# Loading in order of need, preparing weights late, and reordering the opening steps of two expert stages

## What is computed

```
x += tanh(gx[0]) * attention0(c, norm(x))     # 8 heads, rotary keys
x += tanh(gf[0]) * experts0(norm(x))          # top 2 of 8 linear experts
x += tanh(gx[1]) * attention1(c, norm(x))     # 16 heads
x += tanh(gf[1]) * spiking1(norm(x))          # relu^2, then spike counts
x += tanh(gx[2]) * attention2(c, c, norm(x))  # one head, with biases
x += tanh(gf[2]) * experts2(norm(x))          # softmax router, top 2 of 8, gelu, hidden 192
x += tanh(gx[3]) * attention3(norm(x), c, c)  # one head, causal
x += tanh(gf[3]) * quantised3(norm(x))        # 4-bit weights in blocks of 32, 16-bit activations
```

## Time and profile before

| | us |
|---|---|
| three runs: median (lowest to highest) | 2214.97 (2210.58 to 2215.29) |
| the profiled execution | 2211.95 |
| its span | 2210.1 |
| PE busy | 1922.3 (87%) |
| DVE busy | 1670.8 (76%) |
| ACT busy | 1296.7 (59%) |
| POOL busy | 262.2 (12%) |

### The profile page before, as it was taken

How to read it: one execution, slowest core, us unless ns; L and a number is a source line. 1 busy time by engine, 2 the same in 40 slices (tenths; PEclk the granted TensorE clock), 3 DMA queues, 4 the chain that set the end, 5 groups by cost and what they waited for, 6 DMA issues and landing times. The chain is left out here.

```text
span 2210.1 us, 48541 instructions
## 1 busy us (share of the span) xinstructions
PE 1922.3 (87%) x17853; PEld 1474.7 (67%) x17853; DVE 1670.8 (76%) x4753; ACT 1296.7 (59%) x3156; POOL 262.2 (12%) x551
## 2 busy tenths in 40 slices
PE   2999999999978989999989896999999986499708
PEld 2778777777757987877757674677777765244308
DVE  2778777778748968999968695766666578787894
ACT  1777777777752218888856463544544345317844
POOL 0111111111101101111111142000000022200000
PEclk8999999999988998999989897999999998699959
DMA  6111111111105541111100011222122111002452
GB/s 183 45 45 45 45 45 45 45 45 45 45 18 225 221 174 31 31 32 32 31 3 1 10 58 49 84 109 78 77 78 92 63 49 30 1 0 86 171 199 77
DMA packets 114381, 151.53 MB, mean 69 GB/s; under 512 B 46538, under 2 KB 95075, under 8 KB 110051
## 3 DMA queue, kind: packets, MB, share of 16 engines
q1 hardware_dynamic: 108152, 145.72, 20.3%
q10 hardware_dynamic: 5994, 2.70, 0.5%
HBM read 110.11 MB, written 21.50 MB: 60 GB/s over the span
## 5 line engine op out<-in xcount | busy, mean ns | idle before, releaser
L1728 ACT ACTIVATE arena<-banks,b1c 128x512 f32<-128x512 f32 x192 | 131.7, 687 | 168.0 <-PE banks L1603 167.9
L1690 DVE TENSOR_TENSOR arena<-arena 128x512 f32<-128x512 f32 (+1 forms) x256 | 170.6, 685 | 66.1 <-ACT arena L1728 63.0
L606 ACT ACTIVATE arena<-banks,arena 128x128 f32<-128x128 f32 x512 | 180.1, 371 | 1.3 <-DVE arena L556 1.3
L1613 PEld LDWEIGHTS banks<-w2a,arena 128*128 128x128 f32 x1024 | 124.1, 192 | 28.6 <-issue 28.6
L858 PE MATMUL banks<-we,arena 128*128 128x128 f32 x1024 | 131.7, 282 | 4.4 <-DVE arena L922 0.5
L481 PE MATMUL banks<-arena,wk 128*128 128x128 f32 x1024 | 134.6, 286 | 1.1 <-DVE arena L578 1.1
L520 PE MATMUL banks<-wv,arena 128*128 128x512 f32 x256 | 132.0, 598 | 0.0
L481 PEld LDWEIGHTS banks<-arena,wk 128*128 128x128 f32 x1024 | 122.3, 196 | 12.5 <-issue 11.0
L858 PEld LDWEIGHTS banks<-we,arena 128*128 128x128 f32 x1024 | 121.1, 193 | 13.0 <-DVE arena L922 12.8
L1613 PE MATMUL banks<-w2a,arena 128*128 128x128 f32 x1024 | 124.7, 275 | 0.0
L1603 PE MATMUL banks<-arena,w1s 128*128 128x512 f32 x256 | 121.7, 610 | 0.0
(11 more groups left out here) (264 smaller groups left out, 5034.6 us busy)
## 6 DMA issues: line engine op xcount, KB each, us to landing
arena<-coef_scratch SPq DMA_DIRECT2D x32, 2048.0 KB, 7.1
arena<-arena SPq DMA_DIRECT2D x256, 64.0 KB, 2.0
gated_scratch<-arena SPq DMA_DIRECT2D x16, 768.0 KB, 3.2
arena<-gated_scratch SPq DMA_DIRECT2D x16, 768.0 KB, 4.2
arena<-z1T_scratch SPq DMA_DIRECT2D x128, 64.0 KB, 2.3
arena<-in_ctx_turned SPq DMA_DIRECT2D x32, 256.0 KB, 2.9
arena<-in_ctx SPq DMA_DIRECT2D x64, 64.0 KB, 2.1
z1T_scratch<-arena SPq DMA_DIRECT2D x64, 64.0 KB, 1.5
```

Source lines behind the costliest of these rows:

```text
L606: act.activation(prob[:, o, c * P:(c + 1) * P], ps[:, SCORES + o, c * P:(c + 1) * P], ACT.Exp, bias=low[:, o, c:c + 1], accum_out=total[:, ...
L1613: mm = pe.matmul(ps[:, OUT + g.par, j * D:(j + 1) * D], hT[g.par][:, c, j * P:(j + 1) * P], w, start=c == 0, stop=c == CHUNKS2 - 1)
L1690: dve.tensor_tensor(hT[g.par][rows, c, :], hT[g.par][rows, c, :], wide_coef[g.par][rows, e, :], ALU.mult).then_inc(s["scaled"].sem, 1)
L1728: act.activation(hT[g.par][:, c, :], ps[:, HID + c % NHID, :], ACT.Gelu, bias=k.b1c[:, c:c + 1])\
```

## The change

Six things are changed; tile sizes, loops in the steady state and arithmetic stay.

1. **Loads.** SP loads the constants, context tile 0, then wk and wq. ACT loads x tiles 0 to 3, the affine columns (now one transfer), wv, wo, the gates, then x tiles 4 to 15. x tiles 16 to 39, x tiles 40 to 63 and the other 31 weight transfers are issued by SP in attention0, one after each tile's swap. PE and DVE wait for the seven first weight transfers only before their first use; DVE waits for each part of `x` at its first tile; every engine waits for the 31 others at the start of experts0.
2. **Host layout.** Five weights come already transposed, bv already widened, the eight affine vectors and b1 in one array each. Their PE transposes and ACT copies go.
3. **Folded weights** (six matrix products, six copies) are computed on PE and ACT at the start of spiking1.
4. **Dequantising** runs on DVE in experts2, at the end of the step in which group 8 is routed; PE and ACT turn and copy the result at the start of attention3, one matrix after another through one PSUM bank.
5. **experts0, first four steps.** DVE computes the new group's shift before `top_two` instead of after it; ACT copies coefT first, then norms, and only then computes the sigmoids. PE transposes the coefficients before the logits, in all steps.
6. **experts2, first three steps.** DVE runs statistics one step ahead and norms first; the weighing of chunks 0 to 8 comes before the bias sum; PE transposes group 1 early and computes the first three hidden chunks of group 0 one step earlier.

```diff
+        load_x(act, 0)
+        for dst, src in first_act:
+            act.dma_start(dst, src).then_inc(k.first_loaded, 16)
+        load_x(act, 1)
+        ready(act)
...
+    def load_rest(sp, n):
+        if n < 2:
+            load_x(sp, 2 + n)
+        elif n - 2 < len(rest):
+            sp.dma_start(*rest[n - 2]).then_inc(k.rest_loaded, 16)
...
 # attention0, sync
                 for r in range(0, P, 32):
                     sp.dma_start(kr[r:r + 32, :], kc[r ^ 32:(r ^ 32) + 32, :]).then_inc(swapped.at(t), 16)
+                k.load_rest(sp, t.idx)
 # attention0, vector
+                if t.idx == 0:
+                    k.ready(dve)
                 dve.wait_ge(*f["xT_psum"](t))
...
 # Folds.tensor; spiking1 calls it before its steps, Folds.scalar likewise
+        pe.matmul(ps[:, 7, 0:D], w2[:, 2 * D:3 * D], w2[:, 0:D], start=True, stop=True)
...
+        pe.wait_ge(k.folded_sb, 6)
...
+def dequantised_turned(k, pe):
+    pe.wait_ge(k.dequant, 10)
+    for w in range(3):
+        if w:
+            pe.wait_ge(k.turned_sb, w)
+        flat = k.q_deq[:, w].rearrange("p b i -> p (b i)")
+        for c in range(CHUNKS3):
+            mm = pe.transpose(k.psum[:, 7, c * P:(c + 1) * P], flat[:, c * P:(c + 1) * P], k.ident)
+        mm.then_inc(k.turned, 1)
+    pe.wait_ge(k.turned_sb, 3)
...
 # experts0, vector
+            if new and not at(0):
+                shifts(new)
             if far:
                 top_two(far)
+            if new and at(0):
+                shifts(new)
...
 # experts2, tensor
+            if at(3) and not nxt:
+                t_front(pe, at(3))
+            if far and far.idx == 0:
+                hidden(far, 0)
             for q in range(GROUP):
-                if nxt:
+                if nxt and (q or nxt.idx):
                     hidden(nxt, 3 * q)
...
 # experts2, vector
+        def opening(at):
+            nxt, far, new = at(1), at(2), at(3)
+            if new.idx == 0:
+                statistics(new)
+            normalised(new)
+            if far:
+                scores(far)
+                routing(far)
+            if not nxt:
+                statistics(at(4))
+            if nxt:
+                dve.wait_ge(*coef_spread(nxt))
+                for c in (0, 3, 6):
+                    weigh(nxt, c)
+            if far:
+                biased(far)
+            if nxt:
+                weigh(nxt, 9)
...
+            if far and far.idx == G // 2:
+                weights3.vector(dve)
```

More of the change, by code:

```diff
@@ L865, in body @@
                 outputs(g, 0)
+            if g := at(2):
+                pe.wait_ge(*s["coef"](g))
+                if g.has(1):
+                    pe.wait_ge(*s["ct_sb"](g.back(1)))
+                pe.transpose(ps[0:COLS, COEFT, 0:P], coef[g.par], k.ident).then_inc(s["ct_psum"].sem, 1)
             if g := at(3):
@@ L952, in scalar, with shares @@
     def scalar(act):
-        def body(at):
-            if g := at(3):
-                act.wait_ge(*s["gap"](g))
-                if g.has(1):
-                    act.wait_ge(*s["part"](g.back(1)))
-                for n in range(2):
-                    act.activation(share[:, n], gap, ACT.Sigmoid, scale=2.0 * n - 1.0).then_inc(s["share"].sem, 1)
+        def shares(g):
+            act.wait_ge(*s["gap"](g))
+            if g.has(1):
+                act.wait_ge(*s["part"](g.back(1)))
+            for n in range(2):
+                act.activation(share[:, n], gap, ACT.Sigmoid, scale=2.0 * n - 1.0).then_inc(s["share"].sem, 1)
+        def body(at):
             if g := at(2):
@@ L971, in body @@
                                    bias=shift[:, j:j + 1]).then_inc(f["xhat_ready"].sem, 1)
+            if at(3) and not at(0):
+                shares(at(3))
+            if g := at(4):
                 act.wait_ge(*f["xT_psum"](g))
@@ L1691, in weigh, with statistics, normalised, biased @@
                                       ALU.mult).then_inc(s["scaled"].sem, 1)
+        def statistics(g):
+            for j in range(GROUP):
+                d_front.stats(dve, g, j)
+            d_front.aggr(dve, g)
+        def normalised(g):
+            for j in range(GROUP):
+                d_front.xhat(dve, g, j)
+        def biased(g):
+            dve.wait_ge(*s["b2_psum"](g))
+            dve.tensor_tensor(rows_of(g), ps[:, LOGITS, :], rows_of(g), ALU.add).then_inc(s["b2_added"].sem, 1)
+        def opening(at):
[16 more added lines that the diff above has]
+                weigh(nxt, 9)
         def body(at):
             old, nxt, far, new = at(-1), at(1), at(2), at(3)
+            if not at(0) and not old:
+                opening(at)
+                return
             if far:
@@ L1702, in body @@
             if new:
-                for j in range(GROUP):
-                    d_front.stats(dve, new, j)
-                d_front.aggr(dve, new)
+                statistics(new)
             if nxt:
@@ L1709, in body @@
             if new:
-                for j in range(GROUP):
-                    d_front.xhat(dve, new, j)
+                normalised(new)
             if far:
@@ L1744, in body @@
                     act.activation(coefT[0:EXPERTS, :], ps[0:EXPERTS, COEFT, :], ACT.Copy).then_inc(s["ct_sb"].sem, 1)
-            if at(3):
+            if at(3) and (nxt or not far):
                 a_front(act, at(3))
@@ L2140 @@
     arrays, args = {}, {}
[L2141 to L2142 removed]
+    for name, a in laid_out(inputs).items():
         a = np.ascontiguousarray(a)
```

308 lines of the change are left out of this document (156 added, 152 removed).

## The result

The changed kernel takes 2161.65 us (median of 2156.80 to 2165.69), the kernel before 2215.13 us (2210.58 to 2216.57) on the same chip: ratio 0.9766, 95% interval 0.9737 to 0.9794. The forecast, 2170 us, was 8.4 us too high, and its range ended 2.4 us above the result. The profiled executions took 2211.95 and 2156.80 us: 55.1 us less, where the sum had 42.1.

What follows compares the result with a forecast made beforehand. PE was taken as near its ceiling except in a few openings, each bound by a chain of waits. 2211.95 - 31.6 + 1.0 - 4.9 - 9.4 + 2.7 + 0.1 = 2169.85, so 2170 us; range 2164 to 2178.

Steps and rivals of the forecast that it cites:

- Opening, 31.6 us: Program start: loads in order of need bring attention0's first affine step from 41.59 to 10.0 us, gaining 31.6 us.
- The weights didn't bind: Program start: if x moves at full rate beside the constants, the first weights bind and the gain is 32.3 us.
- Loads behind the swaps, +1.0: attention0: loads SP issues after each tile's swap delay swap tails, costing 1 us in all; bounds 0 and 50 us.
- (a): attention0: late x loads hold up the swaps behind them, up to 8 us; 2178 us in all, chance 0.17.
- (d): attention0: every load behind a swap delays its tail, giving back the opening's gain; 2219 us, chance 0.02.
- experts0, 4.9 us: experts0: earlier coefficient copy and broadcast gain 4.9 us in the opening; later DVE-bound steps keep that distance.
- Rival (e): experts0 gains nothing because DVE's new stand for 1/sigma eats the broadcast's gain; 2175 us, chance 0.05.
- experts2, opening, 9.4 us: experts2's opening: early statistics, earlier broadcast and unbroken weighing bring the first output product forward, gaining 9.4 us.
- Rival (b): experts2's opening: PE's clock stays low, losing 3 us of the 9.4; 2173 us, chance 0.08.
- Dequantising, +2.7: Mid experts2: 5.5 us of DVE work delays coefficients and stalls PE, costing 2.7 us.
- Rival (c): Mid experts2: DVE's waits absorb the dequantising, so it hides; 2167 us, chance 0.06.
- Folds 0, turning +0.1: Folding at spiking1's start costs 0; turning dequantised weights at attention3's start fits PE's wait, costing 0.1 us.

Runs made afterwards that it cites:

- the second set of runs: Changed kernel run again without an edit, beside the kernel before: 2161.61 us, ratio 0.9782, against 2207.42 us for the kernel before.
- the kernel with extra products: Changed kernel with experts2's three early hidden chunks put back behind PE's transpose and 14 unused products in their place: 2167.82 us, ratio 0.9791.

## Why the forecast was too high, step by step

The sum took 42.1 us off. The two profiles differ by 55.1, the medians by 53.5 in the first set of runs and 45.8 in the second. Two terms of the sum were too small, experts0 (4.9; measured 8.5 in the first pair of profiles, 7.1 between the mean of all profiles with the old order and that of those with the new) and the opening of experts2 (9.4; measured 12.3 and 13.6), each because I had its mechanism wrong in part. On top of that the sum was made against a single profile, and neither the sum nor the range allowed for the spread of stages that nobody edited.

- *The base.* The sum started from one profile and took every unedited stage as it stood there. Attention1 was 297.8 in it and 290 to 294 in the executions after it, down to 288 in one. "The profiled execution lies inside the three timed runs" says nothing on single stages. In the first pair this is the largest item: 5.5 us, less 1.5 that quantised3 gave back. It is no effect of the change, and the second set of runs puts the change at 45.8.
- *Opening, 31.6 us:* right in mechanism, the size was off by 1.2. The first statistics came at 4.88 instead of 6.0, and the first affine step 3.94 us behind them, at 8.82 instead of 10.0. The rate of 59 GB/s for the first 4.5 us belonged to the old list; with large transfers first it was 165. The weights didn't bind: the last gates landed at 8.74, just in time.
- *Loads behind the swaps, +1.0:* they cost nothing (14.4 us of waits against 13.9). Rivals (a) and (d) fell; that a large transfer holds a swap behind it is real, but no swap stands close enough behind one here.
- *experts0, 4.9 us:* the first weighing came as worked out (22.7 against 22.8 us after the first statistics, the last one of group 0 ending 27.9 us after them against 28.2). What failed is the step "the later steps are bound by DVE's 9 us of work each and keep the distance". It failed in both directions. The granted clock didn't move with the work: it rose 32 to 38 us into the stage in all fourteen profiles without filler products there, so that the first output products, now 6 us earlier, ran at 1.2 GHz for 11 us, and DVE lost 1.30 and 1.49 us waiting for logits. And the steady steps and the drain had 8.9 us of waits for late broadcasts, which I hadn't looked for and which the copy's new place cut to 3.5 (5.2 in the second profile). Up to its first update the stage gained 4.0, in the drain another 4.1. Part of that is again the first profile: the last broadcast of before took 9.4 us, and the drains of the four profiles in the old order took 47.9 to 51.0, those in the new order 46.4 to 48.3. Together it is 7.1 us between the means (178.4 and 171.3), 8.5 in the first pair. Rival (e) fell.
- *experts2, opening, 9.4 us:* the order of events on DVE was right, the size wasn't: 12.3 in the first pair, 13.6 between the means (49.0 and 35.4). Counted from the stage's first statistics, the coefficients were ready at 12.0 instead of 12.6, PE's transpose came at 12.95 instead of 14.9, because the three chunks began at 9.2, not 9.5, and took 3.95 us, not 5.4 (the clock rose in their midst), the broadcast was issued at 16.1 instead of 17.9, landed in 6.74, and DVE's seventeen instructions took 11.1 instead of 11.5. Rival (b) fell for this stage; it was experts0 that ran at the low clock, where I had no rival. What I named as the gain's source (statistics(1) early, the broadcast earlier) is worth 2 to 5 us without the early chunks. What failed is the account of the chunks: the prediction counted their new place only as something in the transpose's way, but it also puts the exp of group 1 early, for which DVE stands 6.00 us in the kernel with extra products instead, and nearly 10 us are gone when the chunks are put back.
- *Dequantising, +2.7:* the stall was 2.41 and the step 2.57 us longer. Rival (c) fell. In nine of ten executions a low clock behind the stall adds 1.7, which the forecast didn't have; that the first profile had none was luck.
- *Folds 0, turning +0.1:* spiking1 took 134.0 us in both, attention3 89.6. Right.

Of the 13 us between sum and profile, 4.0 are the spread of unedited stages, 3.6 experts0, 2.9 the opening of experts2, 2.5 the start with the loads. Between the means of all profiles the opening of experts2 is the largest miss, 4.2 us, and the dequantising, at 4.2 instead of 2.7, goes the other way.

The median of the timed runs lies 4.9 us above the profiled execution, which is why 13 us of error show as 8.4 in the result.

Left open: what decides whether the clock falls behind the stall in mid experts2, and why it falls under a PE that is 93% busy.

## What to carry to other kernels

Before a sum is made against one profile, ask of each unedited stage whether it has waits that vary (late DMA landings between even steps are their mark), and widen the range by them. Where an instruction is moved ahead on an engine, follow it through steady steps and drain as well as through the opening: a transfer that starts earlier in each step also removes the waits at the stage's end, where steps are shorter. And look for what else stands behind a piece of work that you move: here the early chunks gained most on an engine that doesn't compute them. Long housekeeping on a nearly full engine cost nothing here once it was cut to the size of that engine's wait in each step.

## What the hardware showed that I hadn't expected

- The granted clock rose 32 to 38 us into experts0 whether PE's dense work began at +30 or at +24 us. In the changed kernel PE was busy for 10.83 of the 11.00 us from 636.0 to 647.0, at a granted 0.50.
- It stood at 0.52 for 14 us under a PE that was 93% busy. The Trainium skill (TensorE: Matmul & The Clock Gate, The HAM clock gate) says that the default is throttled and activity releases the throttle; that stretch doesn't agree, the early rise in experts2's opening (12 us into the stage, behind the early chunks, instead of 26 to 29) does.
- One wait of 2.4 us in a dense stretch was followed by 3.4 us at 1.2 GHz in nine executions and by none in a tenth.
- The start of a program moved 165 GB/s in its first 4.5 us with large transfers at the head of the lists, 59 with the old list.
